# A three-stage graph layer: the query is computed in the middle stage from kept transposed rows, not in the first

## The reference

```python
xt = xn @ weight                                 # graph part, 4 heads of 64
alpha = softmax(leaky_relu(alpha_l[src] + alpha_r[dst]))      # over the heads
gnn = sum over heads of alpha * xt[dst], copied to all heads
q = elu(xn @ Wq.T) + 1;  k = elu(xn @ Wk.T) + 1;  v = xn @ Wv.T   # 8 heads of 32
attn = q @ (k.T @ v) / max(q @ k.sum(), 1e-6)    # linear attention
x = x + gnn + attn @ Wproj.T + bproj
h = layernorm(x)
logits = h @ gate_w + gate_b                     # 8 experts, the best one is taken
x = x + expert(h)                                # relu(h @ w1 + b1) @ w2 + b2, limited capacity
```

## Time and profile before

| | us |
|---|---|
| median of three timed runs (1677.56 to 1678.15) | 1677.65 |
| profiled execution | 1671.66 |
| its span | 1670.0 |
| TensorE busy | 1403.3 |
| VectorE busy | 1174.8 |
| ScalarE busy | 766.3 |
| GpSimd busy | 625.0 |

### The profile page before, as it was taken

How to read it: one execution, slowest core, us unless ns; L and a number is a source line. 1 busy time by engine, 2 the same in 40 slices (tenths; PEclk the granted TensorE clock), 3 DMA queues, 4 the chain that set the end, 5 groups by cost and what they waited for, 6 DMA issues and landing times. The chain is left out here.

```text
span 1670.0 us, 28940 instructions
## 1 busy us (share of the span) xinstructions
PE 1403.3 (84%) x8633; PEld 1247.3 (75%) x8633; DVE 1174.8 (70%) x3066; ACT 766.3 (46%) x1455; POOL 625.0 (37%) x541
## 2 busy tenths in 40 slices
PE   4999999975776557676562999999999999999995
PEld 4999999964555445455442899999999999999995
DVE  5888888854677677678771567776768676677764
ACT  3545555530111111111112676676767676666763
POOL 1111111116787778778860022221222212222123
PEclk9999999986768778787765999999999999999998
DMA  3444444452343334443334113113131313132000
GB/s 101 119 121 122 121 127 122 119 145 69 100 117 103 105 107 124 116 114 100 101 100 112 72 50 77 50 26 75 49 99 49 81 37 91 49 71 72 24 21 18
DMA packets 119470, 145.20 MB, mean 87 GB/s; under 512 B 58378, under 2 KB 94222, under 8 KB 119301
## 3 DMA queue, kind: packets, MB, share of 16 engines
q1 hardware_dynamic: 67729, 89.23, 18.6%
q0 software_dynamic: 51696, 55.42, 13.0%
HBM read 76.42 MB, written 73.36 MB: 90 GB/s over the span
## 5 line engine op out<-in xcount | busy, mean ns | idle before, releaser
L1248 POOL DMA_INDIRECT out<-o_sb,tok_i x128 | 177.8, 1389 | 608.2 <-issue 608.2
L1446 DVE TENSOR_TENSOR h_lo<-hf,h_hi 128x496 fp32r<-128x496 f32 x256 | 172.8, 675 | 207.9 <-PE psY L1507 88.2
L1507 PE MATMUL psY<-w_hi,h_hi 128*124 128x256 f32 x1024 | 289.7, 283 | 4.3 <-DVE w_lo L1360 4.3
L1507 PE MATMUL psY<-w_hi,h_lo 128*124 128x256 f32 x1024 | 287.5, 281 | 0.0
L1507 PE MATMUL psY<-w_lo,h_hi 128*124 128x256 f32 x1024 | 286.8, 280 | 0.0
L1321 ACT ACTIVATE h_hi<-psH,b_sb 128x496 fp32r<-128x496 f32 x256 | 172.6, 674 | 230.8 <-PE psH L1530 220.6
L1063 PE MATMUL psB<-inv_den,spread_at 128*128 128x125 f32 x400 | 87.7, 405 | 143.5 <-DVE inv_den L848 143.5
L1507 PEld LDWEIGHTS psY<-w_hi,h_hi 128*124 128x124 f32 x1024 | 189.1, 185 | 13.0 <-issue 4.1
L1507 PEld LDWEIGHTS psY<-w_lo,h_hi 128*124 128x124 f32 x1024 | 189.1, 185 | 8.9
L1063 PEld LDWEIGHTS psB<-inv_den,spread_at 128*128 128x128 f32 x400 | 80.9, 309 | 148.2 <-DVE inv_den L848 95.6
L1507 PEld LDWEIGHTS psY<-w_hi,h_lo 128*124 128x124 f32 x1024 | 189.3, 185 | 0.0
(11 more groups left out here) (217 smaller groups left out, 3020.4 us busy)
## 6 DMA issues: line engine op xcount, KB each, us to landing
x_sb<-in_x SPq DMA_DIRECT2D x50, 500.0 KB
wraw<-in_L_ffn_w SPq DMA_DIRECT2D x16, 1024.0 KB, 13.5
expert_rows<-empty POOLq DMA_DIRECT2D x31, 520.0 KB, 8.7
xr<-expert_rows SPq DMA_DIRECT2D x32, 503.8 KB
graph_table<-tab_sb SPq DMA_DIRECT2D x25, 570.3 KB
out<-xd SPq DMA_DIRECT2D x25, 500.0 KB
out<-o_sb,tok_i POOLq DMA_INDIRECT x128
gl<-alpha_l_table,isrc POOLq DMA_INDIRECT x100
```

The costliest lines, as they stand in the source:

```text
L1248: pool.indirect_dma_start(out=out, in_=o_sb[:, par, j, :], in_offset=None, out_offset=bass.IndirectOffsetOnAxis(ap=tok_i[:, par, j:j + 1], ...
L1446: nc.vector.tensor_tensor(h_lo[:, f % 4, :], hf[:, f % 4, :], h_hi[:, f % 4, :].bitcast(F32), ALU.subtract).then_inc(s_hlo_ready, 1)
L1507: ins = nc.tensor.matmul(psY[par][j // 2][0:T3, (j % 2) * D:(j % 2 + 1) * D], hh[:, f % 4, j * T3:(j + 1) * T3], w[:, f, :], start=f == 0 ...
```

## The change

The first stage no longer computes the query. ScalarE copies the transposed rows as they are into xt_all, which takes the place of q_all in SBUF, and xt_lo is made from that copy and not from PSUM. The key is joined in one VectorE operation, min then max, of the exponential and a linear part y + 1 that ScalarE writes (before, VectorE took the minimum first and added 1 in the join).

The second stage computes the query three steps ahead. For step s + 3 ScalarE makes the high part (x_high), VectorE the low part (x_low), and TensorE runs the 12 matmuls (q_mm) at the end of its step, into psB, which den_spread and q_scaled also use. In the next step ScalarE makes the exponential and the linear part (q_parts, first in its step), and VectorE joins them (q_make, behind den_of) into q_t, which has two halves. Three more waits keep psB's users apart. The query's weights stay in SBUF past the first stage. To make room, xg, gt_sb, ctx_t and heads share one buffer, and pr2 and pr4 lie in pr.

```diff
+        wq_hi = sb("wq_hi", [P, KC, D], F32R)
+        wq_lo = sb("wq_lo", [P, KC, D], F32R)
...
+        xt_all = sb_in(late, "xt_all", [P, KC, N])
...
+                        act.activation(xt_all[:, c, bass.ds(s * TS, TS)], psT[c][:, 0:TS], ACT.Copy).then_inc(s_xt_kept, 1)
                     for n in range(2):
                         act.wait_ge(s_k_mm, 2 * s + n + 1)
                         act.wait_ge(s_k_done, 2 * s)
                         act.activation(ek[:, n, :, :], psR[2 + n][0:T, :].rearrange("p (j o) -> p j o", j=2),
                                        ACT.Exp).then_inc(s_ek_exp, 1)
+                        act.wait_ge(s_klo_done, 2 * s)
+                        act.activation(kf[:, n, :, :], psR[2 + n][0:T, :].rearrange("p (j o) -> p j o", j=2),
+                                       ACT.Identity, bias=1.0).then_inc(s_k_lin, 1)
                     for n in range(2):
                         act.wait_ge(s_k_done, 2 * s + n + 1)
                         act.wait_ge(s_g_done, s)
...
                         dve.wait_ge(s_hit_done, KC * s + c + 1)
-                        nc.vector.tensor_tensor(xt_lo[:, c, :], psT[c][:, 0:TS], xt_hi[:, c, :].bitcast(F32),
-                                                ALU.subtract).then_inc(s_lot_done, 1)
+                        dve.wait_ge(s_xt_kept, KC * s + c + 1)
+                        nc.vector.tensor_tensor(xt_lo[:, c, :], xt_all[:, c, bass.ds(s * TS, TS)],
+                                                xt_hi[:, c, :].bitcast(F32), ALU.subtract).then_inc(s_lot_done, 1)
                     if not (isinstance(s, int) and s == 0):
...
-                        dve.wait_ge(s_eq_exp, KC * s + c + 1)
-                        nc.vector.tensor_scalar(eq[:, c, :], eq[:, c, :], 1.0, None, ALU.min).then_inc(s_eq_min, 1)
-                        dve.wait_ge(s_eq_min, KC * s + c + 1)
-                        nc.vector.scalar_tensor_tensor(q_all[:, c, bass.ds(s * TS, TS)], psR[c][:, 0:TS], 1.0,
-                                                       eq[:, c, :], ALU.add, ALU.max).then_inc(s_q_done, 1)
                     for n in range(2):
                         dve.wait_ge(s_ek_exp, 2 * s + n + 1)
-                        nc.vector.tensor_scalar(ek[:, n, :, :], ek[:, n, :, :], 1.0, None, ALU.min).then_inc(s_ek_min, 1)
-                        dve.wait_ge(s_ek_min, 2 * s + n + 1)
-                        dve.wait_ge(s_khi_done, 2 * s)
-                        dve.wait_ge(s_klo_done, 2 * s)
-                        nc.vector.scalar_tensor_tensor(kf[:, n, :, :],
-                                                       psR[2 + n][0:T, :].rearrange("p (j o) -> p j o", j=2), 1.0,
-                                                       ek[:, n, :, :], ALU.add, ALU.max).then_inc(s_k_done, 1)
+                        dve.wait_ge(s_k_lin, 2 * s + n + 1)
+                        nc.vector.scalar_tensor_tensor(kf[:, n, :, :], ek[:, n, :, :], 1.0, kf[:, n, :, :],
+                                                       ALU.min, ALU.max).then_inc(s_k_done, 1)
                     if not last:
                         norm(s + 1, 1 - par)
                     for n in range(2):
...
-                    pe.wait_ge(s_hit_done, KC * s)
+                    pe.wait_ge(s_xt_kept, KC * s)
...
                     pe.wait_ge(s_tab_ready, J * s)
-                    for c in range(KC):
-                        n = 0
-                        for wgt, xt in ((wq_hi, xt_hi), (wq_lo, xt_hi), (wq_hi, xt_lo)):
-                            for kc in range(KC):
-                                ins = nc.tensor.matmul(psR[c][:, 0:TS], wgt[:, kc, c * P:(c + 1) * P], xt[:, kc, :],
-                                                       start=n == 0, stop=n == 3 * KC - 1)
-                                n += 1
...
                     for j in range(J):
-                        if j < KC:
-                            pe.wait_ge(s_q_done, KC * s + j + 1)
-                        else:
-                            pe.wait_ge(s_k_done, 2 * s + j - KC + 1)
...
+                step(0, 0, 0, 3)
+                step(1, 1, 0, 3)
                 with eng.Fori(1, (NS - 3) // 2) as i:
-                    step(2 * i, 0, i, 2)
-                    step(2 * i + 1, 1, i, 2)
+                    step(2 * i, 0, i, 3)
+                    step(2 * i + 1, 1, i, 3)
                 step(NS - 3, 0, (NS - 3) // 2, 2)
...
                     sp.dma_start(tok(out, s, D), xd[:, par, :, 0:D]).then_inc(x_out[par], 16)
-                    if ahead == 2:
+                    if ahead >= 2:
...
             def _(act):
-                for c in range(KC):
-                    act.wait_ge(s_gt_mm, KC)
-                    act.activation(gt_sb[:, c, :], psB[c][:, 0:D], ACT.Copy).then_inc(s_gt_sb_done, 1)
-                for c in range(KC):
-                    act.wait_ge(s_mixw_mm, KC)
-                    act.activation(mix_w[:, c, :], psM[:, KC + c, 0:MW], ACT.Copy).then_inc(s_mixw_set, 1)
+                def x_high(s):
+                    act.wait_ge(s_q_mm, KC * s)
+                    act.activation(xh[:, :, :], xt_all[:, :, bass.ds(s * TS, TS)], ACT.Copy).then_inc(s_xh, 1)
+
+                def q_parts(s, par):
+
+
+                    for c in range(KC):
+                        act.wait_ge(s_q_mm, KC * s + c + 1)
+                        act.wait_ge(s_q_done, KC * s)
+                        act.activation(eq[:, c, :], psB[c][:, 0:TS], ACT.Exp)
+                        if not (isinstance(s, int) and s < 2):
+                            act.wait_ge(s_d_mm, s - 1)
+                            act.wait_ge(s_qp_done, KC * (s - 1))
+                        act.activation(q_t[:, par, c, :], psB[c][:, 0:TS], ACT.Identity, bias=1.0).then_inc(s_q_lin, 1)
 
                 def att_exp(s):
                     act.wait_ge(s_att, NATT * s + 4)
                     act.activation(lex[:, :, :], lex[:, :, :], ACT.Exp).then_inc(s_l_exp, 1)
 
                 def step(s, par, h, ahead):
+                    if ahead > 1:
+                        q_parts(s + 2, par)
                     root(s)
                     logit_exp(s)
+                    if ahead > 2:
+                        x_high(s + 3)
                     if ahead > 0:
                         att_exp(s + 1)
 
+                for c in range(KC):
+                    act.wait_ge(s_gt_mm, KC)
+                    act.activation(gt_sb[:, c, :], psB[c][:, 0:D], ACT.Copy).then_inc(s_gt_sb_done, 1)
+                x_high(0)
+                q_parts(0, 0)
+                x_high(1)
+                q_parts(1, 1)
+                x_high(2)
...
+                def x_low(s):
+                    dve.wait_ge(s_xh, s + 1)
+                    dve.wait_ge(s_q_mm, KC * s)
+                    nc.vector.tensor_tensor(xlo[:, :, :], xt_all[:, :, bass.ds(s * TS, TS)], xh[:, :, :].bitcast(F32),
+                                            ALU.subtract).then_inc(s_xlo, 1)
+
+                def q_make(s, par):
+
+                    for c in range(KC):
+                        dve.wait_ge(s_q_lin, KC * s + c + 1)
+                        nc.vector.scalar_tensor_tensor(q_t[:, par, c, :], eq[:, c, :], 1.0, q_t[:, par, c, :],
+                                                       ALU.min, ALU.max).then_inc(s_q_done, 1)
+
+                def q_scaled(s, par):
 
                     dve.wait_ge(s_mix_mm, 2 * s)
                     for c in range(KC):
                         dve.wait_ge(s_b_mm, KC * s + c + 1)
-                        nc.vector.tensor_tensor(qp[:, c, :], psB[c][:, 0:TS], q_all[:, c, bass.ds(s * TS, TS)], ALU.mult)\
...
+                        q_make(s + 2, par)
                     logits(s)
                     choose(s)
                     if ahead > 0:
-                        q_scaled(s + 1)
+                        q_scaled(s + 1, 1 - par)
                     place(s, par)
                     if ahead > 0:
                         att_scores(s + 1, 1 - par, h + par + 1)
+                    if ahead > 2:
+                        x_low(s + 3)
+                    if ahead > 0:
                         att_sum(s + 1, 1 - par)
                         base_of(s + 1, 1 - par, h + par + 1)
 
+                q_make(0, 0)
+                x_low(1)
                 den_of(0)
+                q_make(1, 1)
+                x_low(2)
                 dve.wait_ge(s_bg_mm, 1)
...
-                def q_ksum(s):
-
+                def q_mm(s):
+
+
+                    pe.wait_ge(s_xh, s + 1)
+                    pe.wait_ge(s_xlo, s + 1)
+                    if not (isinstance(s, int) and s < 2):
+                        pe.wait_ge(s_qp_done, KC * (s - 1))
+                    for c in range(KC):
+                        n = 0
+                        for w, xt in ((wq_hi, xh), (wq_lo, xh), (wq_hi, xlo)):
+                            for kc in range(KC):
+                                ins = nc.tensor.matmul(psB[c][:, 0:TS], w[:, kc, c * P:(c + 1) * P], xt[:, kc, :],
```

(40 more changed lines are left out.)

69 lines of the change are left out of this document (33 added, 36 removed).

## The result

The changed kernel takes 1693.06 us, the median of four runs (1689.54 to 1697.79), against 1677.61 us for the kernel before on the same chip (1677.28 to 1678.15). The ratio is 1.0088, with a 95% interval of 1.0061 to 1.0114: slower by 0.9%. The profiled execution after is the slowest of its four, 1697.79 us, and the one before, 1671.66, is faster than all four of its runs, so their difference of 26 us is larger than the 15.5 us between the medians.

A forecast was written before the change was run, and what follows sets the result against it. First stage bound by TensorE and SP's transfers nearly equally, middle stage by GpSimd's queue and an equally long loop through the gathers. Terms -12 + 17 + 3 = +8 us, from the timed median 1677.65 giving 1685.7; range 1655 to 1702.

The forecast's parts named there:

- both signs of D: Middle stage: den_spread waiting for q_lin, or logits waiting for the root, would show that a new TensorE chain binds.
- The first stage: First stage: step falls from 13.36 to 13.1 us, held there by SP's transfers on five DMA engines; -12 us.
- Rival B: First stage: five engines' turn shrinks to 11.6 us (deciding below 12.8), TensorE's saving stays; -45 there, 1652 us; chance 0.17.
- (f): Ahead of the middle stage's loop: q_mm(2) stands between q_ksum(1) and mix(0), for which the first xd waits; +3 us.
- (a): Middle stage, TensorE: 2.8 us more matmuls per step (5.6 at half clock), covered by idle time ahead of den_spread; cost 0.
- rival D: Middle stage: a new chain on TensorE binds, step 20.9 us, +1.7 us a step, 1710 us in all; chance 0.12.
- (b): Middle stage, ScalarE: about 3.6 us more per step, ahead of root in its queue; cost 0 unless q_mm ends late.
- Case A: The forecast's own sum: middle stage's loop through the gathers sets 19.8 us a step; range 1676 to 1698; chance 0.53.
- (d): Middle stage, VectorE: x_low between att_scores and att_sum delays xd, output, index load and gather; +0.95 us on the loop.
- (e): Middle stage, GpSimd: its DMAs are stretched while VectorE runs operations with two SBUF inputs; +0.45 us per step.
- (c): Middle stage, VectorE: q_make, 1.3 us in front of logits, is covered by 2.55 us idle before att; cost 0.
- the middle stage's term of +20: Middle stage: +17 us for a loop 0.7 us longer in 24 steps, and +3 us at its start.

The follow-up runs named there:

- run 1: Changed kernel with each 125-partition transfer of x and table in the first stage issued as 120 and 5 partitions; 1657.6 us.
- 5: Changed kernel with 10 more matmuls of 500 columns, read by nothing, per middle step between den_spread and the position matmuls; 1681.4 us.
- 6: Changed kernel with ScalarE's root ahead of the query's activations and VectorE's q_make behind choose; 1683.0 us, ratio 0.9991 to 1.0035.
- 9: Changed kernel with root first, q_make behind choose, and no x_low (third product reads the high part of x); 1674.9 us, ratio 0.9965 to 1.0015.
- 7: Changed kernel without any query work in the middle stage, the query being a constant 1; 1665.3 us, ratio 0.9877 to 0.9940.
- 10: Changed kernel with root first, q_make behind choose, and first-stage x and table transfers in 120 and 5 partitions; 1651.9 us.
- 12: Kernel of 10 with 16 more matmuls of 500 columns, read by nothing, per middle step ahead of den_spread; 1653.8 us.

## Why the prediction was right or wrong

It gave 1685.7 with a range of 1655 to 1702 and 0.55 for slower; 1693.1 is inside and on that side. The sum was +8 against +15.5 measured, and the two halves of the miss have different causes. Of its signs of being right, the table writes came (13.0 us apart for 13.1) and the wait for x; the writes of out came 20.6 us apart where it had 19.8, and both signs of D were there.

**The first stage** went as worked out: 13.0 us a step for 13.1, VectorE waiting for x in every step, TensorE no longer full. It gave 8.9 us instead of 12, but made up otherwise: the 22 turns gave 10.4 us where 5.7 was taken (12.89 us each in the mean, 13.0 over the last 20 of them), the first table write came 0.7 us sooner (40.96 for 41.67) and not 3, and behind the 22nd turn the stage took 2.2 us more (39.9 for 37.8) and not 3 less. That the sum is near is in part luck. Rival B's condition did not come about by itself, but its price was right: run 1, which takes the five engines' turn out of the way, shortens the first stage by 45.3 us against the kernel before, where B had 45, and ends at 1657.6 for its 1652. The Trainium skill's rule (DMA: Bandwidth & Descriptors, "Why a DMA increments its semaphore by 16 and not by 1") says that the engines of such a DMA are the largest number up to 16 that divides its slowest dimension. By it 120 partitions run on 15 engines, 0.94 of 16. Run 1 agrees, with shares of 0.93 and 0.89.

**(f), the start of the middle stage**: +3 predicted, 403.19 - 364.53 = 38.66 us against 36.05 before, +2.6.

**(a) is the step that failed.** It put q_mm at nothing while the 4.91 us ahead of den_spread cover it. They did not: den_spread now waits for ScalarE's reads of the same banks (1.15 us in the step shown). But rival D, which the profile then points to, was also priced in the wrong place. It had the query matmuls at half clock, 5.6 us; they took 2.97. The half clock fell on the mix, +2.5 us in the mean (9.2 for 6.7). And it was not worth the 1.7 us a step of D but 10 to 12 us in all: two edits that have nothing else in common, 5 and 6, both end at 1681 to 1683, the one with no slow mix, the other with 11 of 23.

**(b)**, "cost 0 unless q_mm ends late", failed in the same way: q_mm ended 2.7 us behind q_ksum, and root stood behind four activations and a table load. Run 6 took back both the root's place and the pause, and does not tell them apart. Run 5 says more: its ScalarE has the order of the changed kernel, and yet VectorE's reciprocal waits for the root 0.4 us in all 25 steps, where it waited 19.5. So the late root seems to come of the slow mix, which pushes q_mm back. That the two keep each other up (slow mix, late root, pause, low clock, slow mix) fits both runs; no run starts it from one of them.

**Case A fits what lies under it, in its size.** In 5 and 6 the step is 19.9 to 20.0 us; A had 19.8. In medians that is 1682 - 1669 = 13 us of loss in the middle stage, start included, where the sum had 20 (1669 is the kernel before less 9 for the first stage; against the kernel before on their own chip it is 12). Its parts are not borne out. (d), the subtraction, is 0.2 to 0.4 us a step for 0.95. (e), the stretch of GpSimd's DMAs, was nearly absent; the group from 450 to 880 us of the kernel after:

```profile
L720 POOL DMA_INDIRECT gl<-alpha_l_table,isrc x84 | 117.4, 1398 | 59.2 <-issue 29.8 <-DMA idst<-in_dst 29.4
```

That is 1398 ns for 1376, 0.1 us a step over four DMAs where 0.45 was taken. (c), q_make at 0, may be wrong: 10 us by the medians and 14 by the ratios remain between runs 9 and 7 for q_make, ScalarE's and TensorE's work together, and no run divides them. The Trainium skill (SBUF — State Buffer, "Who interferes with whom") has the ports that VectorE shares with GpSimd as an exclusive lock, in which the issue order decides who waits. The trace after shows VectorE waiting no more than the one before: the sum into the buffer of xg takes 1237 ns (L921) for the 1239 of the earlier trace rows. The prediction's aside on this had 0.5 us for x_low and 6 us for the sum, which do not go together (24 x 0.5 is 12); nothing rests on either.

So the middle stage's term of +20 was 24.4 (15.5 + 8.9): 12 to 14 that stay in 5 and 6, where A had 20, and 10 to 12 by a chain that was given a chance of 0.12. The forecast "slower" rested on A, and A would not have been enough for it: 6, the nearest to A without the chain, is at 0.9991 to 1.0035, which can't be told from no change. It needed the chain as well. In that sense the right side was partly luck.

**Open**: what sets the step of 19.8 to 20.2 us in runs 5, 6, 10 and 12. VectorE is busy for 317 of 390 us in 5 and has 50 us of waits, 26 of them for gathered rows, which fits A's loop, and 25 for the position matmuls. Removing x_low from 6 returned at most a third of its time. And the part of the mix in 6 and 10, half of whose mixes are slow, is not known.

## What to carry to other kernels

- Moving work into an engine's idle time is free only if its inputs and the PSUM banks of its outputs are free too. Ask who else writes the bank, and which short operation stands behind the new one in the queue.
- A busy share says nothing of where the pauses lie. Here a pause of 2.5 us ahead of a long operation cost more than one of 4 to 7 us ahead of a short one.
- Count the slow cases and do not go by one step or a median: the median mix of the kernel before is at full clock, and 10 of 23 are not.
- When one stage has two nearly equal bounds, taking work off the one is worth little until the other is widened: 9 us here, and 36 more by splitting 125 partitions into 120 and 5.

## What was not expected of the hardware

- Ten matmuls of 500 columns whose result nobody reads, placed in a pause, made the kernel 12 us faster; the granted clock at the start of the mix stayed at full (mean 0.92 from 450 to 840 us, against 0.79).
- Once fallen, the clock stayed at 0.50 for 10 us, from 657 to 667, with TensorE busy throughout. In the kernel before it was back within 4 us in one step (windows 663 to 667 above) and still at 0.50 at 481 us in another, through den_spread and most of the mix. No run shows why the one is longer.
- A transfer of 125 partitions costs more than the same in two of 120 and 5: 36 us over 25 steps of two such transfers each in the changed kernel, 12 us in the kernel before.
